# One wait of GpSimd's key sums, one subtraction moved up, and a new order for the opening of a cross-attention kernel

## The reference

```python
lat = layer_norm(layernorm(x), ln_lat_g, ln_lat_b)
ctx = layer_norm(ctx_1024, ln_ctx_g, ln_ctx_b)          # 16 x 1024 x 256
q = (lat @ Wq).reshape(b, n, 16, 64)
k, v = jnp.split(ctx @ Wkv, 2, axis=-1)
k = apply_rope(k, cos, sin)      # x1*cos - x2*sin, x2*cos + x1*sin, halves of 32
attn = softmax(clip(q @ k.T * 64 ** -0.5, -11, 11))
x = x + (attn @ v).reshape(b, n, 1024) @ Wo + bo
```

## Time and profile before

| | us |
|---|---|
| three runs | 1250.63, 1251.46, 1252.29 |
| the profiled execution | 1255.13 |
| its span, first to last instruction | 1253.4 |
| PE busy | 1191.6 |
| DVE, ACT, POOL busy | 981.2, 646.7, 700.2 |

### The profile page before, as it was taken

One profiled execution on the slowest core, in us unless ns is written; L12 is line 12 of the kernel. 1 busy time (PEld: TensorE's weight loads), 2 busy tenths in 40 slices (PEclk: granted clock), 3 DMA queues, 4 the chain that ended last, 5 costly groups with the idle time before them and its releaser, 6 DMA issues.

```text
span 1253.4 us, 39825 instructions
## 1 busy us (share of the span) xinstructions
PE 1191.6 (95%) x16268; PEld 1003.6 (80%) x16268; DVE 981.2 (78%) x1954; ACT 646.7 (52%) x1089; POOL 700.2 (56%) x611
## 2 busy tenths in 40 slices
PE   7798999999999999999999999999999999899997
PEld 3576878878877888778878878778878888789997
DVE  6489878878878888888888878778868366668886
ACT  7364455655545545555555545555435233356664
POOL 2374767757667766667767756666434123333333
PEclk8899999999999999999999999999999999999999
DMA  6264656656555665556655656655654441566662
GB/s 228 51 160 109 164 134 149 156 138 153 137 132 140 159 155 138 144 139 160 152 132 141 162 136 149 148 133 132 156 126 110 148 157 36 186 182 194 203 189 68
DMA packets 136173, 181.36 MB, mean 145 GB/s; under 512 B 30316, under 2 KB 96312, under 8 KB 135864
## 3 DMA queue, kind: packets, MB, share of 16 engines
q1 hardware_dynamic: 110552, 150.80, 45.5%
q10 hardware_dynamic: 21360, 23.80, 7.5%
q0 software_dynamic: 4080, 4.22, 1.6%
HBM read 81.93 MB, written 30.56 MB: 90 GB/s over the span
## 4 chain that ended last, share of the span: by engine, by line
PE 87%; issue 3%; DVE 3%; ACT 2%; DMA 2%; POOL 1%; SPq 1%; POOLq 0%; ACTq 0%; DVEq 0%
PE bank L1560 29%; PE bank L1589 27%; PE bank L1546 10%; PE bank L1915 6%; PE bank L1612 3%; PE bank L1719 2%; PE bank L1965 2%; PE bank L1966 1%; PE bank L1967 1%; PE bank L1772 1%; PE bank L1647 1%; PE bank L1815 1%; PE bank L1796 1%; DMA w_two<-in_L_ffn_W_dram 1%; DMA x_slots<-xn_all,slot 1%
## 5 line engine op out<-in xcount | busy, mean ns | idle before, releaser
L1560 PE MATMUL bank<-ct,wk_hi 128*128 128x512 f32 x1024 | 332.7, 407 | 11.0 <-DVE ct L1117 4.2
L1589 PE MATMUL bank<-p_hi,xc 128*128 128x512 f32 x1024 | 316.0, 390 | 0.0
L597 POOL TENSOR_TENSOR kr<-kr,ksw 128x1024 f32<-128x1024 f32 x64 | 154.7, 2417 | 186.8 <-issue 140.3
L1107 DVE TENSOR_TENSOR kw<-bank,stab 128x512 f32<-128x512 f32 x256 | 176.4, 689 | 100.7 <-PE bank L1560 95.3
L1560 PEld LDWEIGHTS bank<-ct,wk_hi 128*128 128x128 f32 x1024 | 192.9, 193 | 53.5 <-issue 8.8
L1589 PEld LDWEIGHTS bank<-p_hi,xc 128*128 128x128 f32 x1024 | 191.8, 188 | 39.8
L1560 PE MATMUL bank<-ct,wk_lo 128*128 128x512 f32 x512 | 204.9, 400 | 0.0
L1589 PE MATMUL bank<-p_lo,xc 128*128 128x512 f32 x512 | 199.2, 389 | 0.0
L779 ACT CAST p_hi<-pr 128x1024 fp32r<-128x1024 f32 x128 | 133.7, 1045 | 88.1 <-DVE pr L1075 87.8
L609 POOL TENSOR_TENSOR xc<-raw,xc 128x255 fp32r<-128x255 f32 x128 | 167.0, 1304 | 1.3 <-ACT xc L742 1.3
L1095 DVE TENSOR_TENSOR p_lo<-pr,p_hi 128x1024 fp32r<-128x1024 f32 x128 | 165.6, 1294 | 0.5 <-ACT p_hi L779 0.5
(11 more groups left out here) (227 smaller groups left out, 1994.9 us busy)
## 6 DMA issues: line engine op xcount, KB each, us to landing
ksw<-kw SPq DMA_DIRECT2D x512, 128.0 KB, 2.3
x_turned<-xt SPq DMA_DIRECT2D x120, 128.0 KB, 3.3
ct_read<-x_turned SPq DMA_DIRECT2D x30, 512.0 KB, 5.1
w_two<-in_L_ffn_W_dram SPq DMA_DIRECT2D x15, 1024.0 KB, 5.1
raw<-in_ctx_dram ACTq DMA_DIRECT2D x56, 256.0 KB, 3.6
x_slots<-fill ACTq DMA_DIRECT2D x32, 258.0 KB, 3.8
w_all<-in_L_ffn_W_dram SPq DMA_DIRECT2D x4, 2048.0 KB, 16.9
wo<-in_L_ffn_W_dram SPq DMA_DIRECT2D x7, 1024.0 KB, 5.0
```

Of the source, the lines that this page charges most:

```text
L597: pool.tensor_tensor(kr_at(j + 2), kr_at(j + 2), ksw[:, i], ALU.add).then_inc(kr_done, 1)
L1107: dve.tensor_tensor(by_tile(kw[:, i, cols]), keys_, by_tile(stab[:, places]), ALU.mult).then_inc(kw_done, 1)
L1560: last = pe.matmul(psK[:, a * 512:(a + 1) * 512], l[:, k, w], ct[:, h % 3, r, k], start=(m == 0), stop=(m == len(parts) - 1))
L1589: last = pe.matmul(psZ[c], xc[:, slot_, l, t, cols], r[:, i, :, t], start=(f == 0 and m == 0), stop=(f == 1 and m == len(parts) - 1), skip ...
```

## The change

On **POOL** the key sum of step j waits for `p_lo_done` to reach j, that is for the low part of step j-1, and no longer for the first half of the keys of step j+4 (or, in the last steps, for a clamp). In the steps before step 0 it comes behind the rstd and the rows' low part of its step, not ahead of them. On **DVE** `half_low` goes ahead of the pair's last `weights_low`, and `blocks_turned(j+1)` is written at the head of the next pair, which leaves its place behind that low part. The **opening** is written out on ACT, DVE and PE: the turn of tile 7 (counted from 1) stands behind keys(0), that of tile 8 behind queries(7, 0), keys(2) behind queries(1, 1); ACT makes the high parts of the last two tiles ahead of the first `normalised`.

```diff
@@ GpSimd
-            def step(j):
+            def keys_summed(j):
                 if there(j + 2):
                     i = j % 2
                     pool.wait_ge(ku_done, 2 * (j + 3))
-                    if j >= 0:
-                        if there(j + 4):
-                            pool.wait_ge(k_ps, 2 * (j + 4) + 1)
-                        else:
-                            pool.wait_ge(clamp_done, j + 1)
+                    wait(pool, p_lo_done, j)
                     pool.wait_ge(sw_ld[i], ((j + 2) // 2 + 1) * 64)
                     pool.tensor_tensor(kr_at(j + 2), kr_at(j + 2), ksw[:, i], ALU.add).then_inc(kr_done, 1)
...
-            for j in range(-5, STEPS):
-                step(j)
+            for j in range(-5, 0):
+                deviations(j)
+                rows_low(j)
+                keys_summed(j)
+            for j in range(STEPS):
+                keys_summed(j)
+                deviations(j)
+                rows_low(j)
@@ ScalarE
-                    opening(g - 10)
-            opening(-3)
+                    context_high(g - 1)
+            rows_high(-4)
+            context_high(6)
+            queries(7, 0)
+            context_high(7)
+            normalised(-4)
+            queries(0, 1)
+            rows_high(-3)
...
-            opening(-2)
-            queries(7, 0)
-            queries(0, 1)
-            opening(-1)
             queries(1, 1)
+            normalised(-3)
+            rows_high(-2)
             queries(2, 1)
+            normalised(-2)
+            rows_high(-1)
             queries(3, 1)
+            normalised(-1)
+            loads(-1)
@@ VectorE
             def two_steps(j):
+                blocks_turned(j - 1)
                 if due(j, 8):
                     added((j - 8) // 4)
...
-                weights_low(j + 1)
-                blocks_turned(j + 1)
                 if half_written(j - 1):
                     half_low(half_written(j - 1))
+                weights_low(j + 1)
@@ TensorE
-            turn_context(6)
             pe.wait_ge(q_act, 6)
             pe.wait_ge(wk_lo_done, 2)
             keys(0)
+            turn_context(6)
             keys(1)
+            queries(7, 0)
             turn_context(7)
-            queries(7, 0)
             queries(0, 1)
+            queries(1, 1)
             keys(2)
-            queries(1, 1)
```

More of the change, by code:

```diff
@@ L590, in step, with deviations @@
                     pool.wait_ge(ku_done, 2 * (j + 3))
-                    if j >= 0:
-                        if there(j + 4):
-                            pool.wait_ge(k_ps, 2 * (j + 4) + 1)
-                        else:
-                            pool.wait_ge(clamp_done, j + 1)
+                    wait(pool, p_lo_done, j)
                     pool.wait_ge(sw_ld[i], ((j + 2) // 2 + 1) * 64)
                     pool.tensor_tensor(kr_at(j + 2), kr_at(j + 2), ksw[:, i], ALU.add).then_inc(kr_done, 1)
+            def deviations(j):
                 for n in stats_at(j):
@@ L605, in step, with rows_low @@
                     pool.tensor_tensor(rstd[:, i:i + 1], ve[:, i:i + 1], consts[:, 2:3], ALU.pow).then_inc(rstd_done, 1)
+            def rows_low(j):
                 if there(j + 4):
@@ L762, in half_high @@
                 act.copy(ct[:, h % 3, 0], low).then_inc(ct_hi_done, HT)
-            def opening(j):
-                if 0 <= j + 9 < ST:
-                    context_high(j + 9)
-                rows_high(j)
-                normalised(j)
-                loads(j)
             def exponential(j):
@@ L882, in _ @@
                     biases()
-                if 0 <= g - 3:
+                if g >= 3:
                     latents_high(g - 3)
                 if g >= 1:
-                    opening(g - 10)
-            opening(-3)
+                    context_high(g - 1)
[6 more added lines that the diff above has]
+            rows_high(-3)
             act.wait_ge(w_last_ld, 32)
             act.activation(w_last[:], w_last[:], ACT.Identity, scale=g_last[:]).then_inc(bias_done, 1)
-            opening(-2)
-            queries(7, 0)
-            queries(0, 1)
-            opening(-1)
             queries(1, 1)
+            normalised(-3)
+            rows_high(-2)
             queries(2, 1)
+            normalised(-2)
+            rows_high(-1)
             queries(3, 1)
+            normalised(-1)
+            loads(-1)
             even_step(0)
@@ L1117, in half_low @@
                 dve.tensor_tensor(ct[:, h % 3, 1], low_as_read(h), ct[:, h % 3, 0].bitcast(F32), ALU.subtract).then_inc(ct_lo_done, HT)
-            def opening(j):
-                if 0 <= j + 9 < ST:
-                    context_low(j + 9)
-                if j <= -4:
-                    shifts(j)
-                keys_turned(j, 0)
-                keys_turned(j, 1)
-                if j > -4:
-                    shifts(j)
-                counted(j)
-                blocks_turned(j)
             def two_steps(j):
+                blocks_turned(j - 1)
                 if due(j, 8):
@@ L1177, in _ @@
             key_weights(1)
-            for j in range(-9, -4):
-                opening(j)
-                if j >= -7:
-                    latents_low(j + 7)
+            for t in range(4):
+                context_low(t)
+                if t >= 2:
+                    latents_low(t - 2)
+            query_weights_low(0)
+            counted(-5)
+            latents_low(2)
             latents_low(3)
-            query_weights_low(0)
+            context_low(4)
+            shifts(-4)
+            counted(-4)
             dve.wait_ge(tab_done, 2)
-            opening(-4)
-            opening(-3)
-            query_weights_low(1)
-            opening(-2)
-            opening(-1)
+            keys_turned(-4, 0)
+            keys_turned(-4, 1)
+            context_low(5)
+            shifts(-3)
+            counted(-3)
+            keys_turned(-3, 0)
+            keys_turned(-3, 1)
+            context_low(6)
+            blocks_turned(-3)
+            context_low(7)
+            query_weights_low(1)
+            shifts(-2)
+            counted(-2)
+            blocks_turned(-2)
+            keys_turned(-2, 0)
+            keys_turned(-2, 1)
             query_weights_low(2)
+            shifts(-1)
+            counted(-1)
+            keys_turned(-1, 0)
+            keys_turned(-1, 1)
             query_weights_low(3)
```

## The result

| | before | after |
|---|---|---|
| median of four runs, us | 1251.05 | 1369.14 |
| lowest and highest | 1246.09, 1252.29 | 1361.14, 1373.17 |
| the profiled execution, us | 1255.13 | 1373.17 |
| its span, us | 1253.4 | 1371.4 |

The ratio is 1.0944, 95% interval 1.0886 to 1.1002: +118 us. Forecast were 1313 us, +61, and a range of 1256 to 1340. The sign and the hold were right; the size was not, and the measured time lies above the range.

A forecast was written before the change was run, and what follows sets the result against it. PE was taken as the bound before, DVE after: +2.53 us a quad over 26 quads, +65.8, less 5 for the opening, makes +61 on 1251.46, so 1313 us; range 1256 to 1340.

The forecast's parts named there:

- the hold: DVE's shift, starting just after GpSimd's key sum, is held off until the sum nearly ends: 2.05 us a step.
- PE as the bound before, DVE's waits as its reserve: Attention loop: PE sets 28.42 us a quad (four steps); DVE can lose its 4.64 us idle before becoming the bound.
- The sum of holds: Loop: 7.85 us of new holds plus 23.1 free work make DVE 30.95 us a quad, +2.53 over PE's 28.42.
- The step that failed: Loop with DVE as bound: its 4.6 us of waiting a quad are used up, PE, exponentials and outputs all early.
- the ring at the outputs: PE's outputs wait for DVE's last key reading, DVE waits for PE in turn; forecast took outputs as early, no cost.
- the low clock: PE's granted clock falling after waits: expected in the opening, 0.84 of full speed on average from 40 to 60 us.
- the third rival: Loop: DVE's 24 us wait for turned blocks stays, POOL's other work adds 17: 1354 us, 1340 and more; chance 0.04.
- Part 2: Half's low part moved ahead of the step's low part on DVE: delays the latter 1.1 us every second pair, cost 0.
- The opening: Rewritten start: scores(0) at 54.7, scores(1) at about 60; worth -5 us, between -8 and 0.
- The tail: From about 850 us on, DVE has spare time and odd steps have nothing to hold: 0.
- What would show it: Profile signs: shifts near 2.1 us, DVE over 95% busy in the loop, PE waiting on DVE some 3 us a quad.

The follow-up runs named there:

- the run behind the shift: Changed kernel, but the key sum waits for the shift that follows the low part, where a step has one: 1257.38 us, ratio 1.0103.
- the new wait: Key sums wait for DVE's low part; as the only change to the kernel before: 1385.62 us, ratio 1.1139.
- the run with the scores first: Changed kernel with PE's outputs behind the pair's two scores and ACT's copy of the outputs behind the two exponentials: 1319.66 us, ratio 1.0598.
- the old wait: Changed kernel with key sums again waiting for the first key bank of step j+4, in the last steps the clamp: 1238.29 us, ratio 0.9950.

## Why the forecast was right in kind and wrong in size

- **PE as the bound before, DVE's waits as its reserve.** PE was the bound. But the forecast read 4.64 us of DVE's idle time a quad as a reserve that any hold may draw on. At the outputs there are 0.9 us.
- **The hold.** Right in mechanism and in order: the sum starts 0.15 us ahead of the shift (forecast 0.22), and a full hold is 2.27 - 0.12 = 2.15 us (forecast 2.05). The Trainium skill (SBUF — State Buffer, "Who interferes with whom") gives that the first one keeps the ports; the trace agrees, 2.27 us for an instruction of 0.12, and so does the run in which the shift is first, 0.121 us. Once a quad the division, not the shift, is the one that is caught (2.51 us instead of 0.57, a hold of 1.94). The forecast's own terms, 2.41 + 0.14 - 0.36 - 0.1, give 2.09 and not 2.05.
- **The sum of holds.** 7.85 us a quad forecast. Measured, against the shift when free (12.4 us, from the run behind the shift), the division at 0.57 and the clamp before: 130.1 + 50.6 + 10.9 = 191.6, or 7.4. The free work was 29.93 - 7.4 = 22.5 instead of 23.1. Together 29.93 instead of 30.95, 27 us too much in 26 quads.
- **The step that failed** is "Its 4.6 us of waiting are used up: PE, exponentials and outputs would all be early." They are not early. 3.15 us a quad are left, 82 us in 26 quads: PE's outputs wait 3.4 us for DVE's last reading, scores and keys stand behind them, and DVE waits for those. Behind that gap PE's clock is mostly low, which makes the waits longer: where it stayed at 1.00 (585.69) DVE idled 1.34 us. So the forecast put two things at nothing in the loop: the ring at the outputs and the low clock that its gap brings. The failed assumption and the sum of the holds together, with 0.06 us of a different base, give 3.15 - 1.02 - 0.06 = 2.07 us a quad, 54 us, all that the measured 119.6 is above the forecast 65.8. Putting the scores ahead of the outputs took 2.25 of the 3.15 us away, and the low clock with them. That PE's gaps, at the low clock, could hold DVE up in turn was in the third rival, and set aside because "DVE is some 2 us a pair behind PE's needs". (By the forecast's own sum DVE is 2.53 us behind in a quad, so 1.3 in a pair.) It was no calculation of the one place at which they meet, and the earlier trace rows with longest waits of 4.0 us for keys had said that DVE's idle time comes in pieces, after PE's own work.
- **The third rival.** The time fell where it said, "1340 and more", and by its condition, but not by its terms: DVE's wait for the turned blocks, which it kept at 24 us, is gone (23.8 us in the 26 quads before, none after).
- **The low clock.** It was expected only in the opening. Now it follows most of the gaps at the outputs; the windows are below.
- **Part 2.** Forecast 0 in the loop. Alone that holds to 0.2%; beside the new wait it spares a hold.
- **The opening.** Step by step close: keys(2) at 45.47 (forecast 46.5), scores(0) at 53.81 (54.7), scores(1) at 59.60 after a wait (60):

```profile
53.81 1.16 PE L1561 MATMUL bank<-qo,kr_third 64*64 64x64 f32 x64
59.60 0.70 PE L1561 MATMUL bank<-qo,kr 64*64 64x64 f32 x16 [4.63 <-POOL kr L593]
```

  With the holds the first outputs started 3.7 us earlier (123.65 instead of 127.31; forecast 5). Alone it is worth 0.0068 x 1245.85 = 8.5 us, between 5.7 and 11.3.
- **The tail.** Forecast 0, measured -3.0 us from the 28th outputs on.
- **What would show it.** The shifts' mean near 2.1 us was not right as put: it is 1.4, since the division takes one hold of four and one is partial. DVE's share of over 95% in the loop was wrong (90%), and that the wait for keys would be gone too (46.2 us left of 71.4). These two marks show the failed step. Wrong too was that GpSimd's "issue" before the sum would turn into a release from DVE's low part: the profile still says "issue" (1.81 us at 611.55), though the sum starts 0.13 us after that low part ends. PE's waits on DVE were right, 3.4 us a quad where some 3 were named, and so were scores(0) and scores(1) at about 55 and 60 us.

## What to carry to other kernels

Slack is a property of a place, not of an average. Before an engine's idle time is spent, find the instruction on the *other* engine that waits for it next, and read how long before it the last input was ready: here 0.9 us, in an engine that idled 4.7 us a quad. Where two engines wait for each other in a ring, a delay beyond that slack is paid at once, and the waits behind it remain. If the delay makes a gap on PE, read the granted clock behind it as well. And where two instructions exclude each other, tenths of a microsecond decide who goes first; a wait on an event just ahead of an engine's work of 0.1 us can hold that work for nearly twenty times its length, and a hold can push the next, unchanged pair over the edge too.

## What the runs showed of the hardware that was not expected

PE's granted clock falls behind most of the gaps at the outputs, 21 of 26. Windows of the kernel after: the gap, the outputs and the two scores, what follows (clock in the third column from the end):

```profile
612.00:617.40 5.40, 2.06 (x10) 1.36 (x8) 5.37 (x10) 0.89 (x2) 3.37 (x4) 1.00 0.79 163
617.40:622.00 4.60, 4.54 (x193) 4.50 (x193) 3.37 (x7) 1.40 (x2) 2.69 (x3) 0.63 0.55 120
622.00:633.00 11.00, 11.00 (x51) 8.92 (x48) 9.84 (x15) 7.55 (x11) 4.85 (x6) 1.00 0.64 138
```

After 3.4 us of idle PE the next 4.6 us run at 0.63 of full speed on average, so mostly at the lower level, and the outputs take 1.66 us instead of 1.16. In the run with the scores first PE idles 1.40 and 0.94 us around the outputs, and here the clock stays:

```profile
619.90:625.50 5.60, 3.26 (x194) 3.02 (x193) 5.28 (x13) 3.14 (x5) 2.42 (x4) 1.00 0.81 182
```

Over the 26 quads the mean is 0.94, and PE's same instructions take 759.80 - 717.96 = 42 us more. So a wait of PE can cost more than its length. How much of the 119.6 us this makes isn't settled: the estimate above, 25 to 43 us, rests on the few gaps behind which the clock stayed. The second surprise is how small the held instruction may be: 128 numbers, 0.12 us, were held for 2.27 us, as long as one of 128x256 (2.51). The readings of the keys, which take one operand from PSUM, keep their pace beside a sum as before: with the old wait they are what a sum mostly runs beside, which fits that it cost nothing there. The hold goes the other way too. GpSimd's low part of the rows got faster by the change, before and after:

```profile
L609 POOL TENSOR_TENSOR xc<-raw,xc 128x255 fp32r<-128x255 f32 x128 | 167.0, 1304 | 1.3 <-ACT xc L742 1.3
```

```profile
L609 POOL TENSOR_TENSOR xc<-raw,xc 128x255 fp32r<-128x255 f32 x128 | 95.1, 743 | 125.7 <-ACT xc L748 125.7
```

Before the change one of them starts at 576.07, while DVE's low part of 575.61 runs until 576.83, and takes 1.35 us instead of 0.74. This is most of the 95 us by which GpSimd's busy time fell.
